# Probabilities transposed by DVE in 32x32 blocks and a trip over DRAM, instead of by PE, in 23 of 32 attention steps

## The reference

```python
# n = layernorm(x); 4 key heads, 8 query heads each, head size 128; per sample 64 query rows, 128 key rows
hidden = concat([context, n], axis=1)
q = (n @ Wq).reshape(b, 64, 4, 8, 128)
k = (hidden @ Wk).reshape(b, 128, 4, 128)
v = (hidden @ Wv).reshape(b, 128, 4, 128)
attn = softmax(einsum('bqhgd,bkhd->bhgqk', q, k) / sqrt(128))
out = einsum('bhgqk,bkhd->bqhgd', attn, v).reshape(b, 64, 4096)
x = x + out @ Wo
```

## Time and profile before

| | us |
|---|---|
| median of 3 runs | 695.19 (695.14 to 695.71) |
| profiled execution, its span (first to last instruction); the page gives no other time of it | 693.9 |
| PE busy | 686.2 (99%) |
| DVE busy | 521.0 (75%) |
| ACT busy | 351.5 (51%) |
| POOL busy | 128.0 (18%) |
| DMA | 90.14 MB, mean 130 GB/s |

### The profile page before, as it was taken

How to read it: one execution, slowest core, us unless ns; L and a number is a source line. 1 busy time by engine, 2 the same in 40 slices (tenths; PEclk the granted TensorE clock), 3 DMA queues, 4 the chain that set the end, 5 groups by cost and what they waited for, 6 DMA issues and landing times.

```text
span 693.9 us, 11059 instructions
## 1 busy us (share of the span) xinstructions
PE 686.2 (99%) x3570; PEld 579.7 (84%) x3570; DVE 521.0 (75%) x1101; ACT 351.5 (51%) x1048; POOL 128.0 (18%) x132
## 2 busy tenths in 40 slices
PE   8999999999999999999999999999999999999997
PEld 6888888888888888888888888888888888788885
DVE  2774966778887888677678776767977658778887
ACT  4454845455543455454355553554645446555553
POOL 0196000000523222012020220210202000022321
PEclk9999999999999999999999999999999999999999
DMA  9997140001425647433342632433643413331101
GB/s 331 361 357 254 64 150 1 1 0 46 141 88 170 202 137 268 149 100 107 108 153 88 214 113 99 151 100 104 197 134 103 145 39 122 94 106 61 46 31 61
DMA packets 70605, 90.14 MB, mean 130 GB/s; under 512 B 4192, under 2 KB 48480, under 8 KB 70560
## 3 DMA queue, kind: packets, MB, share of 16 engines
q1 hardware_dynamic: 65632, 81.71, 35.8%
q10 hardware_dynamic: 4928, 7.87, 3.3%
HBM read 62.29 MB, written 27.26 MB: 129 GB/s over the span
## 4 chain that ended last, share of the span: by engine, by line
PE 93%; DVE 3%; DMA 2%; SPq 1%; ACT 0%; issue 0%; DVEq 0%; ACTq 0%
PE bank L942 24%; PE bank L1014 23%; PE bank L760 15%; PE bank L1137 8%; PE bank L914 6%; PE bank L1193 6%; PE bank L1167 4%; PE bank L751 2%; PE bank L1083 1%; PE bank L879 1%; DMA rawk<-in_L_xattn_Wv 1%; PE bank L845 1%; DMA qbuf<-q_dram 1%; PE bank L835 1%; DVE oT L1644 0%; PE bank L801 0%
## 5 line engine op out<-in xcount | busy, mean ns | idle before, releaser
L1014 PE MATMUL bank<-regA,oT 128*128 128x512 f32 x576 | 135.4, 390 | 0.1
L1014 PEld LDWEIGHTS bank<-regA,oT 128*128 128x128 f32 x576 | 107.8, 188 | 22.5 <-DVE oT L1644 0.2
L1540 ACT ACTIVATE probs<-bank,negmax 128x128 f32<-128x128 f32 x256 | 90.1, 378 | 45.0 <-DVE negmax L2106 45.0
L942 PE MATMUL bank<-xnT,forms 128*128 128x512 f32 x432 | 108.1, 395 | 0.0
L942 PEld LDWEIGHTS bank<-xnT,forms 128*128 128x128 f32 x432 | 79.3, 188 | 15.8 <-DVE qbuf L1860 0.4
L942 PE MATMUL bank<-regC,forms 128*128 128x512 f32 x324 | 83.7, 396 | 0.0
L1228 ACT CAST oT<-bank 128x512 fp32r<-128x512 f32 (+1 forms) x66 | 37.9, 575 | 78.8 <-PE bank L1193 75.8
L942 PEld LDWEIGHTS bank<-regC,forms 128*128 128x128 f32 x324 | 59.1, 188 | 11.3 <-DVE regC L1644 0.2
L760 PE MATMUL bank<-regC,xnT 128*128 128x512 f32 x256 | 68.0, 396 | 0.0
L1228 ACT CAST pT<-bank 128x512 fp32r<-128x512 f32 x64 | 34.5, 594 | 63.7 <-PE bank L1167 63.7
L1137 PEld LDWEIGHTS bank<-k_ring,qbuf 128*128 128x128 f32 x512 | 62.0, 191 | 4.3 <-DMA qbuf<-q_dram 1.9
(11 more groups left out here) (211 smaller groups left out, 1135.1 us busy)
## 6 DMA issues: line engine op xcount, KB each, us to landing
q_dram<-qbuf SPq DMA_DIRECT2D x32, 512.0 KB, 3.1
qbuf<-q_dram SPq DMA_DIRECT2D x31, 512.0 KB, 4.8
raw<-in_L_xattn_Wo SPq DMA_DIRECT2D x4, 2048.0 KB, 10.4
wq_raw<-in_L_xattn_Wq SPq DMA_DIRECT2D x14, 512.0 KB, 4.3
raw<-in_L_attn_Wo SPq DMA_DIRECT2D x6, 1024.0 KB, 8.7
k_ring<-keys_dram SPq DMA_DIRECT2D x32, 128.0 KB, 3.6
v_raw<-vals_dram SPq DMA_DIRECT2D x64, 64.0 KB, 3.5
resid<-in_x SPq DMA_DIRECT2D x4, 512.0 KB, 11.9
```

The source lines that it names most:

```text
L942: last = nc.tensor.matmul(k_bank[:, :], forms[:, p[1], a, i, c, :], right(b)[:, c, :], start=j == 0, stop=j == 5)
L1014: last = nc.tensor.matmul(bank[7][:, :], oT[:, a, h, :], wo_of(g, b, h), start=h == 0 and i == 0, stop=h == GH - 1 and i == 2)
L1540: last = nc.scalar.activation(probs[:, bb, p, :], bank[bb][:, p * P:(p + 1) * P], ACT.Exp, bias=negmax[:, bb, p:p + 1], accum_out=rowsum[: ...
```

## The change

Steps 0 to 22 become `step_turned`; step 23 is `step_between`; steps 24 to 31 are as before, but for layouts.

- ACT writes the exponentials in an order in which each 32 keys of the four blocks of queries lie together (`by_block`), and normalises in eight multiplies of 128 x 128, in place. `probs` has three slots of 512.
- DVE transposes 128 x 512 of a sample in blocks of 32 x 32 (`turn`), from slot 1 + bb to slot bb.
- SP stores both samples to `turns_dram` in four DMAs of 32 partitions (runs of 512 B) and loads them back in one, with keys on the partitions (`pT_raw`, runs of 2 KB). `pT_raw` lies where `pTl` lies, so the load waits for the values of the step before. ACT casts `pT_raw` to `pTh`, DVE subtracts into `pTl`.
- The values of a step are computed at the end of the next one and its projection in the one after (`values_of(*earlier(g, t, 1))`, `project(*earlier(g, t, 2))`); so are the output's casts and subtractions, which move to the start of ACT's and DVE's part.
- The queries have another order of their rows, to fit the turned blocks. `q_dram` is stored in runs of 64 numbers where it was 256. Its loads still have 1024 in a run.
- In the loop before the steps the products 1 and 6 of pair 6 go; step (0,0) has all seven products of that pair.
- SP stores each half of the queries apart, the first before the turned stores, the second behind the values' loads. The output weights come in four loads, in t = 2 to 5, and are cast and subtracted in t = 1, DVE's part in 4 and 4.
- `spare` goes; `u3` and a slot of `probs` serve in its place.

```diff
-    q_dram = nc.dram_tensor("q_dram", (KV, NT, P, GH // 2, 2 * P), F, kind="Internal").ap()
+    SUB = 32
+    turns_dram = nc.dram_tensor("turns_dram", (2, 2 * P // SUB, SUB, P // SUB, 4 * SUB), F, kind="Internal").ap()
+    q_dram = nc.dram_tensor("q_dram", (KV, P, 4 * NT, GH // 4, 2, 2 * SUB), F, kind="Internal").ap()
...
+            def store_turned(g, t):
+                n = 8 * g + t
+                sp.wait_ge(turned, 2 * n + 2)
+                for a in range(P // SUB):
+                    sp.dma_start(turns_dram[t % 2, :, :, a, :].rearrange("c j n -> j c n"),
+                                 probs[a * SUB:(a + 1) * SUB, 0:2, :].rearrange("j b (c n) -> j (b c) n", n=4 * SUB))\
+                      .then_inc(turns_stored, 16)
+            def load_turned(g, t):
+                n = 8 * g + t
+                sp.wait_ge(turns_stored, 64 * n + 64)
+                if not at(g, t, 0, 0):
+                    sp.wait_ge(pv_done, 2 * n)
+                sp.dma_start(pT_raw[:, :, :], turns_dram[t % 2, :, :, :, :]
+                             .rearrange("(b c) j a n -> (c j) b (a n)", b=2)).then_inc(turns_loaded, 16)
...
+            def step_turned(g, t):                                   # SP
+                n = 8 * g + t
+                if not at(g, t, 0, 0):
+                    sp.wait_ge(scores_done, 2 * n)
+                if t == 7:
+                    for f in range(2):
+                        sp.wait_ge(q_stored[f], 64 * g + 128 + 16 * KPAIRS)
+                load_k(g + (t + 3) // 8, (t + 3) % 8)
+                load_q(g + (t + 1) // 8, (t + 1) % 8)
+                p = pair_of(g, t)
+                j = (g + (LEAD - KPAIRS + t // 2) // 4, (t // 2) % 4)
+                if t % 2 == 0:
+                    store_half(*j, p, 0)
+                store_turned(g, t)
+                sp.wait_ge(v_lo, n + 1)
+                load_v(g + (t + 2) // 8, (t + 2) % 8)
+                if t % 2 == 0:
+                    store_half(*j, p, 1)
+                elif has_pair(g, t + 4):
+                    load_pair(p + 2)
+                if at(g, t, 0, 0):
+                    load_pair(LEAD + 2)
+                load_turned(g, t)
+                if 2 <= t < 6:
+                    load_wo(g, t - 2)
...
+            def step_turned(g, t):                                   # PE
+                pair = (pair_of(g, t), (LEAD + (t + 1) // 2) % 2)
+                scores(g, t)
+                if t % 2 or at(g, t, 0, 0):
+                    product_1(pair)
+                    product_6(pair)
+                if at(g, t, 0, 0):
+                    product_2(pair)
+                    product_7(pair)
+                if t % 2 == 0:
+                    product_4(pair)
+                if not (at(g, t, 0, 0) or at(g, t, 0, 1)):
+                    project(*earlier(g, t, 2), t == 1)
+                if t % 2:
+                    product_2(pair)
+                    product_7(pair)
+                else:
+                    product_5(pair)
+                    product_3(pair)
+                if not at(g, t, 0, 0):
+                    values_of(*earlier(g, t, 1))
...
+            scores(2, NT - 1)                                        # PE, step 23
+            project(2, NT - 3, False)
+            values_of(2, NT - 2)
+            probs_transposes(TURN)
+            project(2, NT - 2, False)
+            values_of(2, NT - 1)
...
+            def step_turned(g, t):                                   # ACT
...
+                if begun:
+                    for bb in range(2):
+                        output_high(n - 2, bb)
+                if at(g, t, 0, 0):
+                    direct_high(pair + 1, slot)
+                exponentials(g, t, 0)
+                exponentials(g, t, 1)
+                if t % 2 or at(g, t, 0, 0):
+                    copy_1(pair)
                 for bb in range(2):
+                    act.wait_ge(rrow_ready, 2 * n + bb + 1)
                     for p in range(4):
+                        last = nc.scalar.mul(by_block(bb, p), by_block(bb, p), rrow[:, bb, p:p + 1])
+                    last.then_inc(probs_ready, 1)
+                if not at(g, t, 0, 0):
+                    for bb in range(2):
+                        turned_high(n - 1, bb)
+                    if begun:
+                        act.wait_ge(pv_done, 2 * n - 2)
+                    v_high(g, t)
+                if at(g, t, 0, 0) or t % 2 and has_pair(g, t + 2):
+                    summed_high(pair + 1, slot)
+                if t == 1 and not at(g, t, 0, 1):
+                    act.wait_ge(wo_loaded, 64 * (g - 1) + 16 + 64)
+                    for h in range(GH - 1):
                         act.wait_ge(wo_used, (GH - 1) * (g - 1) + h + 1)
                         wo_high(g, h)
+                    act.wait_ge(proj_done, 8 * g)
+                    wo_high(g, GH - 1)
...
+                if t % 2 == 0 and has_pair(g, t + 3):
+                    direct_high(pair + 2, (slot + 1) % 2)
...
+            def step_turned(g, t):                                   # DVE
...
+                if begun:
+                    for bb in range(2):
+                        output_low(n - 2, bb)
+                for bb in range(2):
+                    maxima(n, bb)
+                if at(g, t, 0, 0):
+                    direct_low(p + 1, slot)
+                elif t % 2 and has_pair(g, t + 2):
+                    direct_low(p + 1, slot)
+                elif t % 2 == 0:
+                    sum_21(p)
+                for bb in range(2):
+                    row_factor(n, bb)
+                if at(g, t, 0, 0) or t % 2:
+                    sum_u2(p)
+                if at(g, t, 0, 0):
+                    sum_11(p)
+                for bb in range(2):
+                    turn(n, bb)
+                if at(g, t, 0, 0):
+                    sum_u3(p)
+                    sum_21(p)
+                else:
+                    for bb in range(2):
+                        turned_low(n - 1, bb)
+                    v_low(g, t)
+                if at(g, t, 0, 0) or t % 2 and has_pair(g, t + 2):
+                    summed_low(p + 1, slot)
+                if t == 1 and not at(g, t, 0, 1):
+                    for h in range(4):
+                        wo_low(g, h)
+                if t % 2:
+                    sum_11(p)
+                if begun:
+                    add_projection(*earlier(g, t, 2))
+                if t % 2:
+                    sum_u3(p)
+                else:
+                    sum_22(p)
+                    sum_u4(p)
+                    sum_12(p)
+                if t == 1 and not at(g, t, 0, 1):
+                    for h in range(4, GH):
+                        wo_low(g, h)
...
+            def step_between():                                      # ACT, step 23
+                n = TURN
+                for bb in range(2):
+                    output_high(n - 2, bb)
+                for bb in range(2):
+                    exponentials(2, NT - 1, bb)
+                for bb in range(2):
+                    turned_high(n - 1, bb)
+                v_high(2, NT - 1)
+                wo_high(KV - 1, 1)
+                for bb in range(2):
+                    output_high(n - 1, bb)
```

More of the change, by code:

```diff
@@ new lines, in step @@
+            def step(g, t, last_group):
+                n = 8 * g + t
+                scores(g, t)
+                divided = not (last_group and t >= 2)
+                front = range(GH - 2) if divided else range(GH)
+                if last_group and t == 2:
+                    router_transposes()
+                project(*earlier(g, t, 1), False, front)
+                if last_group and t >= 2:
+                    expert_transposes(t - 2)
+                if last_group and t >= 3:
+                    expert_weights(t - 3)
+                probs_transposes(n)
+                if last_group and t >= 2:
+                    expert_logits(t - 2)
+                if last_group and t >= 3:
+                    expert_mix(t - 3)
+                if divided:
+                    project(*earlier(g, t, 1), False, range(GH - 2, GH))
+                values_of(g, t)
@@ L1458, in _ @@
             save_latent_values(NT - 1)
-            for p in range(LEAD + 1):
+            for p in range(LEAD):
                 copy_1(p)
@@ L1528, in expert_exp, with exponentials @@
                     .then_inc(e_exp_done, 1)
-            def step(g, t, last_group, first_step=False):
+            def exponentials(g, t, bb):
                 n = 8 * g + t
-                pair = pair_of(g, t) if has_pair(g, t) else None
-                slot = (LEAD + (t + 1) // 2 + 1) % 2
+                act.wait_ge(negmax_ready, 2 * n + bb + 1)
+                if isinstance(n, int) and n > TURN:
+                    act.wait_ge(pT_done, 2 * (n - TURN) - 1 + bb)
+                elif not at(g, t, 0, 0):
+                    act.wait_ge(turns_stored, 64 * n)
+                for p in range(4):
```

(19 more changed lines are left out.)

446 lines of the change are left out of this document (212 added, 234 removed).

## The result

The changed kernel takes **699.32 us** (median of 6 runs, 697.39 to 701.69), the kernel before 695.18 beside it: a ratio of 1.0059, 95% interval 1.0045 to 1.0073. It is 4.1 us slower, where I had forecast 2.4 us faster. The profiled execution took 700.28 us, with a span of 698.5, against 693.9 before: 4.6 more.

The account below looks back on a forecast made before the run. PE was taken as the bound, busy 99% of the span. 693.9 - 20.2 (transposes) + 9.9 (start) + 6.4 (output weights) + 1.5 (step between) = 691.5 us of span, plus 1.3: 692.8 us; range 688 to 698, wider 684 to 702.

Parts of the forecast that it names:

- What bounds the kernel: PE, busy for 99% of the span with 93% of the chain; only work taken off PE or new holes count.
- the gain of 20.2 us: Eight transposes leave PE in 23 steps, 0.87 us each time and 1.06 in (0,0): 20.2 us less.
- The turn: DVE's transpose of 128x512 in 32x32 blocks, in no row before: taken as 0.6 us, 1.34 kept for the range.
- The trip over DRAM: Storing and reloading turned blocks in ordinary steps: hidden, nil, with little to spare at the upper bound.
- rival D: Trip over DRAM late in each odd step, from 62 ns a packet; 718 us at 80 ns; chance 0.08.
- The steps with new output weights: (1,1) and (2,1): DVE's eight subtractions delay the output's low halves, so PE waits 3.2 us, twice: 6.4 us.
- The step between: (2,7): late turned block, then projection waiting for the output's cast and subtraction: 0.7 to 4 us, taken as 1.5.
- The start: Steps (0,0) and (0,1): no projection covers waits for pair 8's weights and the turned block; PE hole of 9.9 us.
- rival A: The forecast itself, 688 to 698 us; chance 0.50.
- Rival B: Holes at the start and output weights mostly close, about 4 of 17.8 us left: 679 us; chance 0.17.
- Rival C: Turn dear, 1.34 us for 0.6: 1.5 us more in each of (0,1), (1,1), (2,1), 697.2 us; chance 0.20.

Follow-up runs that it names:

- experiment 11: The kernel before, with the eight PE transposes of 23 steps done twice: 715.09 us against 695.25.
- experiment 3: Changed kernel, with DVE's last four subtractions of new output weights moved from the end of step t = 1 to behind the maxima of t = 2: 693.49 us.
- experiment 1: Changed kernel, with SP issuing the weight load of pair 8 ahead of the turned stores in step (0,0): 695.16 us.
- experiment 9: Version 8, with the turned block's load in (0,0) issued behind the first query store, ahead of the value loads: 684.20 us, ratio 0.9856 to the kernel before.
- 8: On experiment 3: in (0,0) turned stores first, then pair 8's load, then query store; pair 8's direct forms behind the copy in (0,1): 687.45 us.
- the two edits: Changed kernel with the edits of experiment 1 and experiment 3 together: 688.77 us.
- 4: Changed kernel, with 84 useless transposes on PE between products 2 and 7 of step (0,1): 701.23 us.
- 6: The two edits, with 32 useless PE transposes ahead of product 7 of (0,1) and 6 ahead of the values: median 1.7 us lower than the two edits.
- experiment 10: Experiment 9, with 20 useless PE transposes ahead of the values of (0,0): 684.12 us.

## Why the prediction was wrong

- **What bounds the kernel, and the gain of 20.2 us**: right (experiment 11; ordinary steps of 26.72 us without a wait).
- **The turn**: 0.71 us for an estimate of 0.6. Right in what follows from it.
- **The trip over DRAM**: right, nil in ordinary steps. Two query stores with 256 B runs, alone in the window from 237.5 to 247:

```profile
q1 hardware_dynamic: 4128, 1.05, 50.7%
```

  0.507 x 9.5 us x 16 / 4128 = 18.7 ns a packet, for an estimate of 20. The Trainium skill, "DMA: Bandwidth & Descriptors", "Specifications", has read-modify-write under 512 B; a packet here costs less than half of the 49 ns of one of 1 KB (1.5 times as much for a byte), so no doubling of the estimate shows, and rival D, which needed 62 ns, falls.
- **The steps with new output weights**: 4.3 + 2.5 = 6.8 us for 6.4. Right in sum (confirmed by experiment 3). But the waits are 2.4 and 2.2 us, not 3.2 each; the rest, which I had not counted, is 1.6 us of half clock in one of the two places and a restart of 0.3 us in each.
- **The step between**: 1.2 us (0.5 of it a wait ahead of the projection at 582.6) for 1.5.
- **The start, the step that failed**: "The hole is 278.5 - 268.6 = 9.9 us (8 if the load lands as it did, 12 if later and with dear turns)." It is **16.9 us**: scores (0,2) start at 284.69 in the chain, 15.8 behind 268.9 (the planned 268.6 moved by a start of (0,0) that is 0.3 later), those 0.3, and 0.8 in the scores. Mechanism and place were right, the size was not. The 7.0 us missing are four parts (7.2, as the walk had 0.2 too much behind the cast). 2.7 are the issue at 267.4 in place of 264.7. I had let SP wait only for sum_12, but SP was busy until 267.3: the turned stores went behind a query store that waits for a sum behind both turns, and the four took 3.96 us, for 2.4 to 2.8 at the spacing of my walk. 2.2 are the landing (6.73 us for 4.5), 1.5 the values at half clock, 0.8 the scores. Product 7 at half clock costs 1.5 as well, but it hides behind multiplies, cast and subtraction. Seen from PE, the start has 12.1 us of idle time (1.8, 9.5 and 0.8), not far above my 9.9, and matmuls that take 3.9 us longer than in the flow (1.55, 1.54 and 0.80), for which I had nothing. The place in the queue is shown by experiments 1 and 9; why the landing took 6.7 us is not shown, and three executions with the same order of issues have 6.3, 6.7 and 8.2.

The corrected terms, put into the sum: 693.9 - 20.2 + 16.9 + 6.8 + 1.2 = 698.6 us of span, measured 698.5. The two smaller terms together are off by 0.1 us, so this one term turns the sign. The measured 699.32 lies above rival A's 688 to 698 and inside the wide range of 684 to 702. Experiment 1 takes back 4.2 us with the one load issued earlier, enough to bring the kernel to the time before; 8 and 9 another 4.6 beyond the two edits by putting turned stores and their load in front. Rival B (4 of 17.8 us left) would have been 679; experiment 9 shows that most of that can be had, but by an order that the change didn't have. Rival C's time, 697.2, was near the result by chance: the turn wasn't dear.

Left open: how much time the half clock costs at the start. The fillers (experiments 4, 6, 10) restored the clock and gained nothing or an amount within the spread. The traces of 4 and 6 put it at 1.3 to 1.4 us of the 3.9 us of longer matmuls, the rest being covered by the wait for the turned block; no median confirms that. At the projection of (1,2), where nothing else was late, it cost 1.6 us.

## What to carry to other kernels

Where a change adds transfers to an in-order queue, write that queue out instruction by instruction, with the issue time of each and what each waits for: a store that waits for a late sum, and 4 us of issuing behind it, decided the sign here while every average had room. The first steps, before the pipeline has other work to cover a wait, deserve their own walk. And price a wait of PE with what can follow it: here a wait of 2.2 to 2.4 us brought 0.3 us of restart each time, and in one of two places another 1.6 us at half clock.

## What the runs showed of the hardware

- Four stores of 128 KB from 32 partitions each took SP 3.96 us to issue in (0,0) of the changed kernel, with a 256 B query store just ahead of them, and 1.86 us in experiment 9, without it.
- Waits of PE did not all end in half clock: behind 1.83 us ahead of product 7 of (0,0) in the changed kernel the six matmuls took 1.66 us, full speed with a start-up; behind 2.42 us ahead of the projection of (1,2) 24 took 7.32 us in place of 5.44. In experiment 10 the scores (0,2) took 3.28 us behind waits of 0.44, 0.16 and 1.37 us, with a granted clock of 0.50 from 278 to 280.
- One and the same wait can end either way. In experiment 1 the projections of (1,2) and (2,2) have the waits of the changed kernel (2.42 and 2.23 us), but there the first runs at full clock (5.73 us) and the second at half, the reverse of the changed kernel (7.32 and 5.74):

```profile
392.50 5.73 PE bank L1098 x24
...
501.90 7.36 PE bank L1098 x24
```

- A multiply by a column of factors, one of eight on ACT, is 430 ns on the page; eight in a row take 2.34 us by the chain, 0.29 each.
